# Six batches under one mask, token tiles in an order of their own, and a batch's scores begun on the first tile

## What is computed

```python
x = x + tanh(g_xattn[0]) * align(ctx, layernorm(x))            # dynamic time warping over 1500 context rows
x = x + tanh(g_ffn[0])   * memory(layernorm(x), w_q, keys, w_down, w_up)
x = x + tanh(g_xattn[1]) * attention(layernorm(x), ctx, ctx)   # 16 heads of 8
x = x + tanh(g_ffn[1])   * experts(layernorm(x))               # the best 2 of 8
...
# align: a table of path costs, the cheapest path walked back through it,
# and the context rows that the path pairs with a token are summed for it
# memory: 8 heads pick one of 8192 experts each by two half keys (argmax)
h = gelu(einsum("bnd,bnhkd->bnhk", x, w_down[indices])) * relu(scores)
return einsum("bnhk,bnhkd->bnd", h, w_up[indices])
```

## Time and profile before

| what | us |
| --- | --- |
| median of 3 runs | 514.64 |
| the profiled execution's own time | 514.87 |
| its span, first to last instruction | 513.1 |
| what lies around the span | 1.77 |
| busy: PE, DVE, ACT, POOL | 422.1, 369.7, 255.5, 91.3 |

### The profile page before, as it was taken

The page is one execution under the profiler, slowest core; times in us unless marked ns, Lnnn a source line. Parts: engine busy times, 40 slices in busy tenths (PEclk is TensorE's granted clock), DMA queues, the critical chain, the costliest instruction groups (busy, mean ns, idle before and its releaser), DMA issues.

```text
span 513.1 us, 10171 instructions
## 1 busy us (share of the span) xinstructions
PE 422.1 (82%) x4013; PEld 252.1 (49%) x4013; DVE 369.7 (72%) x967; ACT 255.5 (50%) x442; POOL 91.3 (18%) x123
## 2 busy tenths in 40 slices
PE   8998777886888887100888899999999999989996
PEld 5444334444565673000334466666666666654443
DVE  7768999997666786866686888988889884462222
ACT  4565866765222681100103456666666667645443
POOL 1013333311000001777330000210210210200000
PEclk9999999989999999655789999999999999999999
DMA  7600574435423003992161005384483482000000
GB/s 279 248 0 24 176 211 133 141 125 146 131 60 114 9 1 71 221 234 83 50 150 36 1 3 113 71 181 92 93 182 83 102 273 59 1 1 1 0 1 18
DMA packets 28941, 50.28 MB, mean 98 GB/s; under 512 B 2470, under 2 KB 18622, under 8 KB 28894
## 3 DMA queue, kind: packets, MB, share of 16 engines
q1 hardware_dynamic: 27070, 45.96, 33.4%
q0 software_dynamic: 1536, 3.67, 2.9%
q10 hardware_dynamic: 288, 0.00, 0.0%
HBM read 39.96 MB, written 9.45 MB: 96 GB/s over the span
## 4 chain that ended last, share of the span: by engine, by line
PE 47%; DVE 31%; issue 10%; POOL 7%; ACT 2%; DMA 2%; DVEq 0%; POOLq 0%
PE banks L1635 7%; PE banks L1611 7%; POOL arena L569 7%; PE banks L1666 5%; PE banks L1708 5%; DVE work L1271 5%; DVE mx L1034 5%; PE banks L1723 4%; DVE arena L1245 4%; DVE arena L1295 2%; PE banks L1328 2%; DVE mx L1042 2%; PE banks L1479 2%; DVE work L1240 2%; PE banks L1332 2%
## 5 line engine op out<-in xcount | busy, mean ns | idle before, releaser
L1034 DVE TENSOR_REDUCE mx<-banks 112x1 f32<-112x500 f32 x168 | 107.1, 675 | 16.2 <-PE banks L1611 16.0
L777 ACT ACTIVATE arena<-banks 128x896 f32<-128x896 f32 x96 | 87.9, 917 | 48.1 <-PE banks L1666 47.5
L1350 PE MATMUL banks<-steps,one 128*128 128x500 f16 (+1 forms) x188 | 53.3, 377 | 33.9 <-DVE hcol L982 33.9
L1635 PE MATMUL banks<-arena 128*32 128x112 f32 (+1 forms) x1536 | 57.1, 265 | 1.5 <-ACT arena L777 0.8
L1611 PE MATMUL banks<-ctxT,arena 96*112 96x500 bf16 x144 | 54.7, 393 | 3.8 <-DVE mx L1034 1.1
L1635 PEld LDWEIGHTS banks<-arena 128*32 128x32 f32 (+1 forms) x1536 | 33.7, 109 | 21.5 <-issue 18.9
L1271 DVE SCALAR_TENSOR_TENSOR work<-twice,banks,arena 128x202 f32<-128x202 f32 x68 | 29.5, 434 | 18.6 <-PE banks L1479 18.6
L1350 PEld LDWEIGHTS banks<-steps,one 128*128 128x128 f16 x188 | 19.0, 103 | 48.0 <-issue 38.4
L1245 DVE TENSOR_TENSOR_SCAN arena<-work,arena 128x100 f32<-128x100 f32 x70 | 37.2, 531 | 7.3 <-ACT work L640 5.0
L1666 PEld LDWEIGHTS banks<-arena,ctxT 99*128 99x128 bf16 (+1 forms) x576 | 37.5, 103 | 9.9 <-issue 2.1
L1666 PE MATMUL banks<-arena,ctxT 99*128 99x112 bf16 (+1 forms) x576 | 41.2, 213 | 0.0
(11 more groups left out here) (272 smaller groups left out, 734.0 us busy)
## 6 DMA issues: line engine op xcount, KB each, us to landing
ctxT<-key_parts SPq DMA_DIRECT2D x36, 375.0 KB, 7.0
key_parts<-arena SPq DMA_DIRECT2D x32, 281.2 KB, 3.0
ctxT<-in_ctx_T SPq DMA_DIRECT2D x12, 500.0 KB, 8.8
arena<-key_parts SPq DMA_DIRECT2D x12, 375.0 KB, 7.8
ctxT<-in_ctx_nat SPq DMA_DIRECT2D x5, 750.0 KB
arena<-in_ctx_nat SPq DMA_DIRECT2D x3, 750.0 KB
arena<-in_L_ffn_W SPq DMA_DIRECT2D x1, 2048.0 KB, 9.7
arena<-in_fold_w SPq DMA_DIRECT2D x1, 768.0 KB, 5.9
```

The costliest lines, as they stand in the source:

```text
L777: nc.scalar.activation(Pt[0:rows, g % 2, :].rearrange("p (a n) -> p a n", a=2), banks[0:rows, 2 + 2 * (g % 2):4 + 2 * (g % 2), 0:HQ // 2], ...
L1034: nc.vector.tensor_reduce(mx3[:, b % 2, u // NPIECE, u % NPIECE:u % NPIECE + 1], ps[k % 2][0:2 * NJ, 0:PIECE], AX_X, ALU.max).then_inc(s_m ...
L1350: nc.tensor.matmul(bank[:, 0:cols], one16[:, :], steps16[:, 0:cols], start=True, stop=True, skip_group_check=True)
L1635: last = nc.tensor.matmul(ps[6 + b % 2][q:q + 32, o:o + 2 * NJ], vals[0:rows, v0:v0 + 32], Pt[0:rows, g % 2, 2 * t * NJ:2 * (t + 1) * NJ], ...
```

## The change

- **Marks.** POOL makes only the left difference. DVE compares the other neighbours itself (`L1346`) and makes one set of marks of 500 columns from POOL's difference (`L1348`). Both stand one step into the next block, not at the end of it.
- **Masks.** The first pair of batches has 15 masks of 112 columns, the other six batches together 15 masks of 336. Sums start slab by slab.
- **Tiles.** Alignment, layer norms, choice, down, queries: each tile goes alone, in a hand-written order. Gathers wait for all sums (`s_ex` 2) and for their tile's choice.
- **Up.** The weighted sum over experts moves from DVE to PE: ACT writes 8 diagonal matrices for a tile (`diagonals`), and PE adds 8 products (`up`), already transposed.
- **Batch 0's scores.** They begin when tile 0's queries are laid. Maxima are taken two pieces at a time, 12 of them, between the other tiles' steps.
- **Late query rows.** Queries of tiles 1 to 3 are split by POOL and laid within the main loop, in four groups each, at the chunks of `ROWS_AT`; ACT copies all rows.

The diff, cut to its core:

```diff
+    ROWS_AT = {(t - 1, (2 if t == 1 else 6) + pair): (t, pair) for t in range(1, 4) for pair in range(4)}
+    MASKED = ((0, 2), (2, NB))
+    PM_SLOTS = 10
...
-                nc.gpsimd.tensor_tensor(three(gaps[k % 2][:, 0:N_B]), R_slot(t, n, 1, C), R_slot(t, n, 0, C), ALU.subtract)
-                nc.gpsimd.tensor_tensor(three(gaps[k % 2][:, N_B:2 * N_B]), R_slot(t + 1, n, 0, C),
-                                        three(mring[:, t % (2 * TB) * C:(t % (2 * TB) + n) * C]), ALU.subtract
+                nc.gpsimd.tensor_tensor(three(gaps[k % 2][:, 0:N_B]), R_slot(t, n, 1, C), R_slot(t, n, 0, C), ALU.subtract
                                         ).then_inc(s_gap, 1)
...
+            pool.wait_ge(s_ex, 2)
             for t in range(4):
                 pool.wait_ge(s_idx, t + 1)
...
+            pool.wait_ge(s_oT, 4)
+            for t in range(1, 4):
+                lo, hi = TILE[t]
+                n0, n1 = 2 * t * TT, 2 * (t + 1) * TT
+                pool.wait_ge(s_qc, t)
+                step(nc.gpsimd.tensor_tensor(
+                    Qw.rearrange("p (b a q) -> p b a q", b=2, a=2),
+                    xc[:, lo:hi].rearrange("p (b q) -> p b q", q=NJ).unsqueeze(2).broadcast_to([P, 2, 2, NJ]),
+                    hm[:, :].unsqueeze(1).unsqueeze(3).broadcast_to([P, 2, 2, NJ]), ALU.mult))
+                step(nc.gpsimd.tensor_copy(QS[:, 0, n0:n1], Qw))
+                step(nc.gpsimd.tensor_tensor(Qw, Qw, QS[:, 0, n0:n1], ALU.subtract))
+                step(nc.gpsimd.tensor_copy(QS[:, 1, n0:n1], Qw))
+                nc.gpsimd.tensor_tensor(QS[:, 2, n0:n1], Qw, QS[:, 1, n0:n1], ALU.subtract).then_inc(s_qsp, 1)
+                pool.wait_ge(s_qsp, t)
...
+            def diagonals(t):
+                act.wait_ge(s_hm, t + 1)
+                if t >= 1:
+                    act.wait_ge(s_oT, t)
+                for h in range(NHK):
+                    last = nc.scalar.activation(diag[:, h, :], ident[0:TT, 0:TT], ACT.Copy, scale=hcol[:, t, h:h + 1])
+                last.then_inc(s_dg, 1)
...
+            act.wait_ge(s_ebc, 2)
+            path_starts(0, 0, NS)
+            path_starts(1, 0, 4)
+            path_sums(0)
+            path_starts(1, 4, 8)
+            act.wait_ge(s_fold, 1)
+            nc.scalar.activation(fold[:, :], ps[3], ACT.Copy).then_inc(s_fold_sb, 1)
+            path_starts(1, 8, 12)
+            deviation(1)
+            path_starts(1, 12, NS)
+            path_sums(1)
+            path_sums(2)
+            token_rows(0)
+            deviation(2)
+            path_sums(3)
             deviation(3)
+            table_of(4, ACT.Gelu)
+            act.wait_ge(s_pz, 1)
+            own = ident[:, :].rearrange("p (m r) -> p m r", r=G)
+            for c, (_, qx) in enumerate(PRODUCTS):
+                last = nc.scalar.activation(picks[:, :, qx, c::len(PRODUCTS)], own, ACT.Copy)
+            last.then_inc(s_picks, 1)
+            gelu(0)
+            diagonals(0)
+            table_of(5, ACT.Sqrt)
+            token_rows(1)
             deviation(4)
+            token_rows(2)
+            deviation(5)
+            table_of(6, ACT.Gelu)
+            gelu(1)
+            diagonals(1)
+            token_rows(3)
+            query_rows(0, 0)
+            query_rows(0, 1)
+            query_rows(0, 2)
+            gelu(2)
+            diagonals(2)
+            query_rows(0, 3)
+            gelu(3)
+            diagonals(3)
+            table_of(7, ACT.Sqrt)
+            deviation(6)
+            deviation(7)
+            copy_queries(1)
+            copy_queries(2)
+            deviation(8)
...
+            def masks(g, s0, s1):
+
+                b0, b1 = MASKED[g]
+                for s in range(s0, s1):
+                    if g == 1 and s == PM_SLOTS // 2:
+                        ve.wait_ge(s_ex, 1)
+                    if g == 1 and s >= PM_SLOTS:
+                        ve.wait_ge(s_slab, s - PM_SLOTS + 1)
+                    ve.wait_ge(s_am, g * NS + s + 1)
                     nc.vector.scalar_tensor_tensor(
...
+            def first_maxima(j):
+
+                ve.wait_ge(s_s1, 2 * (j + 1))
+                b0 = 2 * (j % 2)
+                nc.vector.tensor_reduce(mx3[:, 0, :, :].rearrange("p m i -> p (m i)")[:, 2 * j:2 * j + 2],
+                                        banks[0:2 * NJ, b0:b0 + 2, 0:PIECE], AX_X, ALU.max).then_inc(s_mx, 2)
...
+            def tiles():
+                masks(0, 0, NS)
+                masks(1, 0, 5)
+                ve.wait_ge(s_gate, 1)
                 add_alignment(0)
+                masks(1, 5, 7)
                 centre(1)
+                masks(1, 7, 11)
                 scale(1)
+                masks(1, 11, NS)
                 ve.wait_ge(s_tabs, 5)
                 choose(0)
+                add_alignment(1)
                 centre(2)
+                add_alignment(2)
                 scale(2)
+                centre(3)
+                choose(1)
+                down(0, 0, NHK // 2)
+                add_alignment(3)
+                scale(3)
+                down(0, NHK // 2, NHK)
+                weigh(0)
+                centre(4)
+                choose(2)
+                down(1, 0, NHK)
                 add_memory(0)
+                scale(4)
+                centre(5)
+                weigh(1)
+                scale(5)
+                choose(3)
+                split_queries(0)
+                down(2, 0, NHK)
                 add_memory(1)
+                first_maxima(0)
+                weigh(2)
+                first_maxima(1)
+                centre(6)
+                down(3, 0, NHK // 2)
+                first_maxima(2)
+                first_maxima(3)
+                down(3, NHK // 2, NHK)
+                add_memory(2)
+                first_maxima(4)
+                weigh(3)
+                first_maxima(5)
+                centre(7)
+                first_maxima(6)
+                scale(6)
+                first_maxima(7)
+                scale(7)
+                first_maxima(8)
+                add_memory(3)
+                first_maxima(9)
+                first_maxima(10)
+                centre(8)
+                first_maxima(11)
...
-                nc.vector.tensor_scalar(moves[k % 2][:, :], gaps[k % 2][:, :], 0.0, None, ALU.is_lt).then_inc(s_nv, 1)
+                t, n = CODES[k]
+                nc.vector.tensor_tensor(three(never_of(k)), R_slot(t + 1, n, 0, C),
+                                        three(mring[:, t % (2 * TB) * C:(t % (2 * TB) + n) * C]), ALU.is_lt)
+                nc.vector.tensor_scalar(left_of(k), gaps[k % 2][:, 0:N_B], 0.0, None, ALU.is_lt).then_inc(s_nv, 1)
...
+                if t == 2 * TB - 2:
+                    signs_of(0)
+                if t % TB == 1 and 2 * TB <= t < (SIDE + 1) * TB:
+                    signs_of(t // TB - 1)
...
+            def up(t):
+                pe.wait_ge(s_dg, t + 1)
+                for h in range(NHK):
+                    last = nc.tensor.matmul(ps[4 + t][:, 0:TT], gath[:, t, h, D:], diag[:, h, :],
+                                            start=(h == 0), stop=(h == NHK - 1), skip_group_check=True)
+                last.then_inc(s_oT, 1)
...
+            sums(0, 0, NS)
+            sums(1, 0, 2)
+            sums_transposed(0)
+            sums(1, 2, 3)
+            mean_once(1)
+            sums(1, 3, 5)
+            variance_of(1)
+            sums(1, 5, 9)
             pe.wait_ge(s_fold_sb, 1)
+            tokens(0)
+            sums(1, 9, NS)
             sums_transposed(1)
+            sums_transposed(2)
+            keep_busy(ps[3], 2)
+            mean_once(2)
+            keep_busy(ps[3], 2)
             variance_of(2)
+            mean_once(3)
+            keep_busy(ps[3], 3)
             tokens(1)
+            variance_of(3)
+            sums_transposed(3)
+            keep_busy(ps[3], 4)
+            mean_once(4)
+            tokens(2)
+            keep_busy(ps[3], 3)
+            variance_of(4)
+            up(0)
+            mean_once(5)
+            variance_of(5)
+            tokens(3)
+            queries(0)
+            keep_busy(ps[0], 3)
+            up(1)
             pe.wait_ge(s_picks, 1)
+            for pair in range(3):
+                query_rows(0, pair)
...
+            first_scores(0)
+            first_scores(1)
+            mean_once(6)
+            first_scores(2)
+            query_rows(0, 3)
+            first_scores(3)
+            up(2)
+            variance_of(6)
+            first_scores(4)
+            first_scores(5)
+            mean_once(7)
+            first_scores(6)
+            variance_of(7)
+            first_scores(7)
+            up(3)
+            first_scores(8)
+            queries(1)
+            first_scores(9)
+            queries(2)
+            first_scores(10)
+            mean_once(8)
+            first_scores(11)
+            variance_of(8)
+            pe.wait_ge(s_qc, 2)
+            pe.wait_ge(s_qpa, 4)
...
+                    if g == 0:
+                        queries(3)
```

(2 more changed lines are left out.)

508 lines of the change are left out of this document (234 added, 274 removed).

## The result

The changed kernel took 487.62 us in the median of 4 runs (485.85 to 488.57), the kernel before 514.18 on the same chip: ratio 0.9478, 95% interval 0.946 to 0.9497. The forecast was 491, its range 482 to 501. The profiled execution took 487.19 us.

The account below looks back on a forecast made before the run. Serial stages (DVE's table stage, POOL's gathers, the way to the main loop) were taken to bind, then PE in the main loop. 514.87 - 2 - 29.7 + 6.6 + 1 = 490.8, so 491 us; range 482 to 501.

Parts of the forecast that it names:

- marks, first scan to first hop: Table stage: one POOL subtraction ends the scan's wait; -7.2, +8.7 and -3.7 us, sum -2.2, bounds -3 and +5.
- first hop to first gather: Masks to first gather: PE's sums end last, gathers begin near 192.4 us, not 205.27; -12.9 us.
- first gather to tile 1's rows: Tiles 0 and 1: 16 gathers from 192.4 us, 1.3 apart, last issued at 211.9 and landing near 218.5.
- these to idx of tile 3: DVE's steps from tile 1's down to tile 3's choice: 12.1 us with 2.0 for hops, so 230.6.
- idx of tile 3 to the split: Tile 0's queries, first scores, maxima and tile 3's steps: from 230.6 us to 260.1, against 289.8 before.
- loop, longer by: Main loop: late query rows on PE +6.6 us (bounds 3 and 8), lower clock at entry +1 (0 to 3).
- The rival that the wait stays: Table stage: POOL's one subtraction still holds a scan, so -2 becomes +5; 498 us, chance 0.08.
- Landing: Tile 1's rows land some 6.6 us after their last gather's issue, beside key-part loads, as tile 0's took 6.7 before.
- The rival that rows land sooner: Tile 1's gathers land in 2.6 us, not 6.6, and all that follows moves by 4; 487 us, chance 0.15.
- The rival that the long queues hinder each other: Tiles' order: DVE and ACT wait for each other in hand-written queues, some 8 to 12 us; 501 us, chance 0.07.
- The rival that PE stays at the lower clock: Through the maxima and the loop's first chunks PE stays low, 3 to 6 us more; 496 us, chance 0.17.
- Gathers stretched: Rival of slower gathers while DVE works: at 2.3 us each, not 1.3, the gain is gone (515 us); chance 0.03.

Follow-up runs that it names:

- the second subtraction alone: Changed kernel plus a second 500-column subtraction on POOL in 11 of 12 table-stage blocks, result unread and no semaphore waiting; 495.83 us, ratio 0.9643.
- the doubled rows: Changed kernel with the twelve late groups of query rows (tiles 1 to 3) issued twice on PE, 72 products more; 493.96 us, ratio 0.9608.
- the ten products: Changed kernel plus ten unused products of 448 columns on PE ahead of the transposes of batch 0's maxima; 488.33 us, ratio 0.951.

## Why the prediction was right

**The chain.** The earlier trace rows called the gathers serial from 205.27 us, and everything up to the split hung on them. It was so: counted as stretches of the path, the steps come out nearly term by term.

| from, to | forecast, us | measured, us |
|---|---|---|
| marks, first scan to first hop | -2.2 (taken as -2) | -2.48 |
| first hop to first gather | -12.9 | -13.1 |
| first gather to tile 1's rows | 26.1 | 23.8 |
| these to idx of tile 3 | 12.1 | 11.8 |
| idx of tile 3 to the split | 29.5 | 29.6 |
| loop, longer by | 6.6 + 1 | 7.9 |

**Marks.** The reading of the earlier trace rows, a scan held off by POOL, is shown by the second subtraction alone, which nobody waits for and which costs 0.80 a block. As forecast, all 70 scans of the changed kernel take 0.42 or 0.43. The rival that the wait stays would have been worth 5 us and did not come.

**Masks.** First gather forecast near 190 (192.4 less 2), measured 189.11, and PE's sums end last as forecast. A mask of 336 columns takes 0.50 (2.00 for four), where 0.51 was taken without a row. The sentence that masks at 0.57 would not change it is not tested as such, and there was little room: the choice ends at 187.98, the last sum at 188.79. With 5 us more on DVE the choice ends last, and the gather moves by 3.2.

**Landing, the one term that was off.** Tile 1's rows were given 6.6 us, from tile 0's 6.7 in the earlier trace rows; it took 4.6. That 2.0 is most of the 3.4 us between forecast and result; half a us of marks and the 0.6 of an earlier start are the rest of note. The rival that rows land sooner was half right: the time is at its 487, but by 2.0 of its 4 us and these smaller terms, so the agreement with its number is luck. Nor is the 4.6 a constant: over the kernels whose key loads stand as in the changed one, profiled executions show 4.3 to 7.8 us, and 2.7 to 2.8 where the loads are held, near the 2.64 of the earlier trace rows. So the forecast's cause, the loads, is shown for tile 1's rows, and 6.6 lies within what they do. What moves the landing between 4.3 and 7.8 stays open.

The gap on POOL before tile 3 is 3.86 us, not some 6: its choice came earlier with tile 1's rows, and POOL had waited 1.76 for tile 2's index already.

**Tiles' order.** Moving the maxima behind the memory layer costs 9.9 us at the split, so the overlap of attention's start with tile 3's gathers is about that part of the gain. The rival that the long queues hinder each other (501) would have shown in DVE's waits: those after tile 1's down are 2.86 and 1.46 for ACT and 1.59 for PE, 5.9 in all, and between the last down and the last maximum 1.46, where the forecast had 1.2. Up on PE and the diagonals lay beside the maxima as said. The rival that PE stays at the lower clock (496) came only in part: the query rows run at 0.2 us a product (3.01 for 15), as taken in the sum, and the clock is 1.00 from 231.5 to 238, then 0.70 and 0.88 to 246 and 254. But behind the first maximum DVE waits for no scores.

**Late rows and clock.** The loop is 7.9 longer where 7.6 was said, and that the two are so near is in part luck. By the doubled rows 72 products are 6.7 of it, by the price of 0.1 from the earlier trace rows they were 7.2 less the slack of the first chunks. Some 0.9 are waits without releaser (1.5 against 0.6 before), which the forecast did not have, and what remains for the clock is near 0.4. But the rows at the entry show 0.62 and 0.58 up to 261.58 and 0.42 and 0.36 behind, and by the ten products the lower level costs some 1.3 us there, near the 1 of the forecast. The two figures agree if the first 72 products cost some 0.9 less than the second 72, as the slack of 0.8 in the first chunks would have it; no run tells that apart.

**Gathers stretched.** The rival of the other sign needed 2.3 us a gather; from first to last of tiles 0 and 1 they are (208.28 - 189.11) / 15 = 1.28 apart, with DVE at work through most of it. Two readings behind this rival were off. Not one gather in 32 was that long but two: another takes 1.97 (231.42), beside DVE's product of a down (`L980`), not beside casts. And the casts beside the one of 2.00 (218.75, `L973`) were copies of 128 columns that the changed kernel has on ACT, not the split's of 896, so "a quarter as wide" compares with others. In the changed kernel the gather beside tile 0's casts takes 1.02 (226.22), and the longest, 1.49 (213.44), lies beside a down again. That casts hold gathers up is not shown here.

## What to carry to other kernels

When a serial stage blocks everything behind it, look for the first piece of its result with which the next stage can start, and count what each engine would fill its waits with: here that was worth some 10 of 27.7 us (the maxima put last). A term that rests on one landing time should carry the spread of that landing over executions, and a transfer put off to clear one landing is to be followed to the next landing it meets. Work handed to the engine that bounds a later stage comes back there at its full price.
